# A mixed image and text block on one core: one run of scatters, unread products where TensorE waits, and a later place for three gates

## What is computed

```python
h = concat([tok(x), txt(x_txt)], axis=1)              # 32 x 68 x 256
h = h + attn(layernorm(h))
h = h + ffn(layernorm(h))
# attn
u = x @ W_x.T + b_x;  g = sigmoid(x @ W_g.T + b_g)     # hidden 512
u = u * g + conv3(u) * (1 - g)
dt = clip(softplus(x @ W_dt.T + b_dt).mean(axis=(0, 1)), 1e-3, 2)
A = -softplus(A_raw);  A_d = exp(A * dt);  B_d = (A_d - 1) / (A + 1e-6) * B_ssm
new = A_d * carry + B_d * u_t;  y_t = new . C_ssm      # 16 states, 68 steps
out = layernorm(x + y @ W_out.T + b_out)
# ffn: softmax router on a normalized row, the two best of four experts
hid = relu(layernorm(h @ w1[e]));  expert_out = hid @ w2[e]
out = layernorm(sum over the two best of weight * expert_out)
```

## Time and profile before

| | us |
|---|---|
| median of 3 runs (505.38 to 506.0) | 505.75 |
| the profiled execution | 506.89 |
| its span on the core | 505.1 |
| PE busy, share of the span | 440.4, 87% |
| DVE | 335.9, 66% |
| ACT | 299.7, 59% |
| POOL | 152.3, 30% |
| mean granted clock of TensorE | 0.935 |

### The profile page before, as it was taken

The page is one execution under the profiler, slowest core; times in us unless marked ns, Lnnn a source line. Parts: engine busy times, 40 slices in busy tenths (PEclk is TensorE's granted clock), DMA queues, the critical chain, the costliest instruction groups (busy, mean ns, idle before and its releaser), DMA issues.

```text
span 505.1 us, 9872 instructions
## 1 busy us (share of the span) xinstructions
PE 440.4 (87%) x3094; PEld 360.9 (71%) x3094; DVE 335.9 (66%) x980; ACT 299.7 (59%) x669; POOL 152.3 (30%) x255
## 2 busy tenths in 40 slices
PE   8989988697799999998998869999899999999500
PEld 5769967465678878886776657888778888888300
DVE  6876567788989125335787985876574666666584
ACT  2854368378866465225564533887596777877341
POOL 2000000000000000002245884874677645454322
PEclk9999999699799999988999958999999999999855
DMA  8981099800049942967212221232232243242262
GB/s 179 180 229 47 32 295 314 241 1 1 0 100 208 191 113 67 243 194 206 66 42 65 94 74 53 75 103 77 86 104 85 77 123 118 70 146 78 72 213 80
DMA packets 58734, 59.92 MB, mean 119 GB/s; under 512 B 25369, under 2 KB 51261, under 8 KB 57405
## 3 DMA queue, kind: packets, MB, share of 16 engines
q1 hardware_dynamic: 54236, 48.68, 37.1%
q0 software_dynamic: 3552, 9.74, 5.1%
q10 hardware_dynamic: 896, 0.89, 0.6%
HBM read 34.50 MB, written 24.80 MB: 117 GB/s over the span
## 4 chain that ended last, share of the span: by engine, by line
PE 70%; DVE 12%; ACT 8%; issue 5%; DMA 2%; another core or an unknown queue 1%; SPq 1%; POOL 0%; DVEq 0%; POOLq 0%; ACTq 0%
PE bank L1016 13%; PE bank L863 9%; PE bank L431 8%; PE bank L433 8%; PE bank L432 7%; PE bank L929 6%; PE bank L1006 3%; PE bank L883 3%; PE bank L911 2%; PE bank L923 2%; PE bank L988 2%; PE bank L954 1%; DVE spj L1380 1%; DMA got<-expert_y 1%; PE bank L933 1%
## 5 line engine op out<-in xcount | busy, mean ns | idle before, releaser
L1016 PE MATMUL bank<-w,hr 128*128 x320 | 76.1, 380 | 2.9 <-DVE ysb L1641 2.6
L1016 PEld LDWEIGHTS bank<-w,hr 128*128 128x128 f32 x320 | 59.9, 189 | 13.6 <-issue 4.5
L642 POOL MEMSET ones<- 2x128 f32 x1 | 0.2, 206 | 214.3 <-PE bank L898 214.3
L1214 ACT ACTIVATE hr<-bank,gsel 128x128 f32<-128x128 f32 x160 | 60.0, 460 | 0.2 <-PE bank L1006 0.2
L717 POOL DMA_INDIRECT expert_y<-ysb,toid x40 | 42.9, 1072 | 52.9 <-DVE ysb L1641 37.9
L863 PE MATMUL bank<-Tb,U 68*32 68x68 f32 x1024 | 46.3, 360 | 0.1
L863 PEld LDWEIGHTS bank<-Tb,U 68*32 68x32 f32 x1024 | 41.1, 141 | 3.4 <-issue 2.9
L1626 DVE BATCH_NORM_STATS2 bsth<-bank 128x6 f32<-128x512 f32 x40 | 27.7, 693 | 20.4 <-PE bank L433 15.0
L929 PE MATMUL bank<-Wo,yT 128*128 128x256 f32 x136 | 36.8, 418 | 2.4 <-ACT yT L1029 2.1
L669 POOL DMA_INDIRECT sorted_x<-x2s,slot x34 | 33.7, 991 | 16.7 <-issue 9.3
L1206 ACT ACTIVATE hn<-bank,nmrh,rsh 128x512 f32<-128x512 f32 x40 | 31.1, 779 | 10.0 <-DVE nmrh L1635 8.0
(11 more groups left out here) (296 smaller groups left out, 1154.7 us busy)
## 6 DMA issues: line engine op xcount, KB each, us to landing
Tb<-ssm_kernels SPq DMA_DIRECT2D x16, 680.0 KB, 9.2
sorted_x<-zpad SPq DMA_DIRECT2D x6, 1419.0 KB, 13.8
xg<-sorted_x SPq DMA_DIRECT2D x40, 129.0 KB
got<-expert_y SPq DMA_DIRECT2D x17, 256.0 KB, 3.7
XI<-in_x_dram SPq DMA_DIRECT2D x12, 288.0 KB, 5.4
h0r<-h_spill SPq DMA_DIRECT2D x17, 128.0 KB, 2.6
out_dram<-acc SPq DMA_DIRECT2D x17, 128.0 KB
w1raw<-in_L_ffn_w_dram SPq DMA_DIRECT2D x4, 512.0 KB, 15.5
```

The costliest lines, as they stand in the source:

```text
L1016: mm = pe.matmul(bank[6][:, 0:D], hr[:, i % 3, c, :], w2[:, bass.ds(expert[i], 1), c, :].rearrange("p o n -> p (o n)"), start=(c == 0), st ...
L1214: last = act.activation(hr[:, i % 3, c, :], bank[3 + i % 2][:, c * P:(c + 1) * P], ACT.Relu, scale=gsel[:, i, 0, c:c + 1], bias=gsel[:, i, ...
```

## The change

There are four edits. The number of DMAs and of products that are read stays the same.

1. In the sort, the tiles of a first-part group now lie 0.1 times as far apart for `scat` (`RUN`), so that each group's eight indirect DMAs are next to each other on POOL.
2. In the tile stage, `fill` gets new places (`FILLS`, and 3 ahead of the waits of `yT` 0 and `out` 0), and the 16 ahead of the first `b1` become 8.
3. `idle`, the same thing with other weights, stands 20 times before `project_dt(4)` and 14 times in chunk 1.
4. In chunk 1, ACT makes `u_parts` of blocks 0 and 1 and all four exponentials before its first `gate`, which leaves one table load where there were three; TensorE makes u of block 3 before g of block 2.

```diff
+        RUN = 0.1
@@ place_of
             elif kind == "scat":
-                n, late = RG[group_of(i)][-1] // 2, i - RG[group_of(i)][0]
+                first_part = group_of(i) < PART0_GROUPS
+                n, late = RG[group_of(i)][-1] // 2, (i - RG[group_of(i)][0]) * (RUN if first_part else 1)
@@ TensorE
+            pe.wait_ge(sem("v_init"), 4)
+            idle(bank[1], 20)
             for q in range(AHEAD, HC * NB):
                 project_dt(q)
             for step in C_STEPS:
+                if step == ("proj", 1, 2):
+                    project(1, 2, "u")
+                    project(1, 3, "u")
+                    pe.wait_ge(sem("dt_read"), HC * NB)
+                    idle(bank[4], 14)
+                    project(1, 2, "g")
+                    continue
                 if step[0] == "proj":
-                    project(step[1], step[2])
+                    project(step[1], step[2], "g" if step == ("proj", 1, 3) else "ug")
                     continue
...
+            FILLS = {("yT", 13): 2, ("out", 13): 3, ("x2T", 10): 7, ("yT", 14): 7, ("lgm", 11): 2, ("yT", 15): 2}
             for kind, i in order("pe"):
+                if (kind, i) in FILLS:
+                    fill(bank[3], FILLS[kind, i])
                 if kind == "yT":
                     if i == 0:
+                        pe.wait_ge(sem("w1_hi"), 1)
+                        fill(bank[3], 3)
...
                 elif kind == "out":
+                    if i == 0:
+                        fill(bank[3], 3)
...
                     if i == 0:
                         pe.wait_ge(sem("slot"), PART0_GROUPS)
-                        fill(bank[3], 16)
+                        fill(bank[3], 8)
@@ ScalarE
             u_parts(1, 0)
-            gate(1, 0)
-            act.preload_act_table_set("natural_log_exp_and_others")
+            u_parts(1, 1)
             for j in range(HC):
                 act.wait_ge(sem("adt"), j + 2)
                 act.activation(Eb[:, j], Eb[:, j], ACT.Exp).then_inc(sem("powers"), 1)
-                if j == 1:
-                    u_parts(1, 1)
             for step in C_STEPS:
                 if step[0] == "proj":
                     if (j, nb) not in ((1, 0), (1, 1)):
                         u_parts(j, nb)
-                    if (j, nb) != (1, 0):
-                        gate(j, nb)
+                    gate(j, nb)
```

More of the change, by code:

```diff
@@ L819, in _, with project @@
                     project_dt(step[1])
-            def project(j, nb):
+            def project(j, nb, kinds="ug"):
                 n0, w = BLOCKS[nb]
@@ L825, in project @@
                 for wt, first, done, read in ((1, 0, "u_mm", "v_init"), (2, 2, "g_mm", "gate")):
+                    if done[0] not in kinds:
+                        continue
                     if c >= 2:
@@ L839, in _, with idle @@
                 project(0, nb)
+            def idle(ps, count):
+                for _ in range(count):
+                    pe.matmul(ps[:], WT[0][0][:, 0, 0:P], WT[0][0][:, 0, :], start=True, stop=True)
+            pe.wait_ge(sem("v_init"), 4)
+            idle(bank[1], 20)
             for q in range(AHEAD, HC * NB):
@@ L956, in _ @@
                     if two(i):
-                        if i == 0:
-                            pe.wait_ge(sem("w1_hi"), 1)
                         fill(bank[3], 2)
```

## The result

The kernel after takes **497.29 us** (median of 4 runs, 496.07 to 498.21) where the one before takes 505.56 us in the same comparison (504.4 to 506.0). The ratio is 0.9847 with a 95% interval of 0.9817 to 0.9877: 8.3 us less (6 to 9 by the interval), where 7.3 were forecast.

A forecast was written before the change was run, and what follows sets the result against it. TensorE bounds the kernel from 306.3 us on, but earlier waits for DVE and ACT at partly half clock. Gates -2.2, twenty products +1.4, head -1.7, tile stage -4.8 sum to -7.3 us: 498.4 from 505.75, range 494.8 to 502.8.

The forecast's parts named there:

- The bound: From 306.3 to 476.8 us TensorE is busy at full clock, so time gained before 306 should reach the end.
- The twenty products: Before project_dt(4): 20 products delay the dt stage; 1.4 us lost, between 0 and 2.4 depending on the clock.
- The gates: Chunk 1: ACT's exponentials before its gates save two table loads; kT 2.2 us earlier, 14 unread products cost nothing.
- The Toeplitz loads: Behind kT in chunk 1: DVE's copy to kt becomes late itself, leaving 1.9 us earlier for these loads.
- The head: Tile stage's start: six unread products keep the clock up for the first two out; 1.7 us gained, or 0.
- The tile stage: Up to the first b1: 3.5 us from 16 to 8 and full clock, 1.3 from scatters; 4.8, from 3.4 to 5.7.
- the 1.3 of the forecast: Scatters in one run: DVE's r1 14 comes 0 to 2.1 us earlier, taken as 1.3 with faster out's 0.4 inside.
- The scheme of POOL's two runs: POOL in the tile stage: eight scatters, four additions, eight scatters, seven additions back to back to 299.5 us.
- The lock of DVE and POOL: Tile stage: by the skill, each DVE instruction waits for one POOL addition at most, 0.73 us; stage gain then 5.7.
- Only the 16 less 8 count: Rival: detour before dt costs 2.4 us, head's clock falls as before, r1 14 no earlier; 502.4 us, chance 0.21.
- The slower rival: Unread products become the bound if TensorE is at half clock near 290.4; 509.2 us, chance 0.07.
- Absorbed: Rival: POOL's table ends when it did, so TensorE's gain ends in waits for toid or gsel; 505.7 us, chance 0.04.

The follow-up runs named there:

- no_run: The kernel after with RUN = 1, so the first part's scatters are spread again: 499.01 us, ratio 0.9859 to before.
- no_twenty: The kernel after without the 20 unread products ahead of project_dt(4), the 14 in chunk 1 kept: 494.88 us, ratio 0.9815 to before.
- gates_alone: The kernel before with only ACT's new order in chunk 1 and u of block 3 moved, no unread products: 500.81 us, ratio 0.9942.
- after_again: The kernel after, unchanged, measured and profiled a second time as a control: 497.36 us, ratio 0.9861 to before.
- fills_alone: The kernel before with only the tile stage's unread-product edit (new places, 16 to 8), scatters still spread: 501.00 us, ratio 0.9924.
- the second set: The four runs no_run, no_head, no_front and early_add, measured beside runs of the kernel before at 506.57 us.
- early_add: The kernel after with the 20 products ahead of q = 8, POOL's h0b 12 ahead of the second scatter run, h0b 13 first behind: 499.28 us, ratio 0.9857.
- the three fastest kernels: The kernel after with the 20 ahead of q = 8 (493.01 us); also 2 products for the 8 (492.86); also two POOL additions moved (491.78).
- no_head: The kernel after without the 3 and 3 unread products ahead of yT 0 and out 0: 501.36 us, ratio 0.9895 to before.
- no_front: The kernel after with FILLS empty, without the 23 unread products in the waits of tiles 10 to 15: 503.07 us, ratio 0.9919.

## Why the prediction was right, and where it was not

**The bound.** "What comes earlier at 306 should come earlier at the end": confirmed by the pair without a standstill, 7.40 us at the first `b1` and 7.07 at the last product. Of the stretches at half clock ahead of it, though, the prediction names four, and the trace has a fifth, from 220.9 to 224.3 us; the second profile of the kernel before lacks it.

**The twenty products: the term was mis-sized.** The mechanism, the first short projection (88.8 forecast, 88.89 measured), the start of `q` = 8 (95.2; 95.33), the gap (3.7; 3.65) and the clock's fall behind it came as written. The size did not: +1.4 was taken between 0 and 2.4, and in the two pairs of profiles it is +2.5. The step that failed is the credit for `q` = 8 at half clock ("would lose some of these" waits): DVE waits 1.21 us for its first result in the kernel after the earlier trace rows, so nothing was won back by that wait. What is won back hangs on how long the clock stays low: in `no_run`, with 3.4 us and not 6.8, the stage ends 1.1 us sooner than in the kernel after, which is the forecast's +1.4. Against `no_twenty` the detour costs 2.9 us in the profiles and 1.6 to 2.3 by the ratios. The term's value lies between its middle and its upper end, mostly near the latter.

**The gates: mis-sized the other way.** Forecast -2.2, measured -4.3 from the end of dt to `kT`. Two steps of the sum were off. The last gate, counted from the end of dt, ends 2.9 us earlier than before, and not 1.8: the prediction priced a block on ACT at 1.33 + 0.70 = 2.03 us, and a gate follows the last after 1.82 (in the kernel before it was 1.80), and the part ahead of them was 0.5 us too long as well. The turns behind it take 1.4 us less than before, since they run at full clock, where the prediction had 0.7 at most for the clock and left it out of its 2.2. The 1.8 does stand in `gates_alone`, where the last gate starts 1.7 us earlier, but by luck: there ACT waits 0.93 us for products at half speed, which the forecast did not have. Of the 4.3, ACT's order gives 2.9 and the 14 products 1.5. The prediction priced them at "nothing": it asked only what they cost and not what the clock without them would do. The two table loads are 1.28 us each as before. The Trainium skill's 2.66 us per switch (ScalarE: Activation LUTs, "What ACT_TABLE_LOAD costs") would have made ACT's part 4.9 us; the isolated run shows 2.9 in all, so the trace still does not agree with it.

**The Toeplitz loads** were to be the next late thing (DVE late with its copy, 1.9 us left for them). DVE is late as forecast (waits 0.16 us, and is 1.74 us earlier from the end of dt). But TensorE's first `ssm` step keeps the whole 4.3 us, since TensorE's own queue stood ahead of it and not the load: the first 680 KB landed at 151.55 us and the step began at 152.17. Some of the 4.3 us is given back in the steps behind: from `kT` to `yT` 0 the kernel after takes 0.4 us more than before in the first pair (whose before had 3.4 us at half clock there) and 1.2 in the second. That loss stood in no term. So the forecast for `yT` 0, 0.8 us earlier (1.4 lost, 2.2 won), is met (1.4 and 0.7) by three errors that cancel: 2.5 lost, 4.3 won, 0.4 to 1.2 given back. The loss comes with the 14 products: every profile that has them takes 88.7 to 89.4 us there, `gates_alone` 88.0. Two new waits of TensorE are in it, 0.66 us ahead of a turn at 208 us and 0.29 ahead of an `ssm` step at 217 in `after_again`; the trace names no releaser for them, and the rest is not settled.

**The head.** Forecast -1.7; measured -1.8 and -1.4. The reason given, that the six products keep the clock up, is not confirmed: two profiles without them had the clock up too.

**The tile stage.** Forecast -4.8 (3.5 for 16 to 8 and the clock, 1.3 for the run). From `yT` 13 to the first `b1` it gained 5.7 and 6.0 us, and lost 1.0 and 0.65 between the head and `yT` 13: -4.7 and -5.4. `fills_alone` gives 3.9 of it (3.5 and the 0.4). The kernel after is 1.8 us better there, but the run of scatters taken back alone costs only 0.9 (`no_run` takes 16.93 us from `yT` 13 to the first `b1`, after 16.04), so the 1.3 of the forecast lies between two measurements, of which the one that isolates the run is the lower, and 0.66 go off ahead of `yT` 13. Eight products take 1.85 us (1.84 forecast), the turn 0.75 (0.69). The scheme of POOL's two runs came out as drawn, with tile 12's addition late and DVE waiting for it. Counted from the first scatter (271.18 and 268.37), the second pair of `ln1b` starts after 26.0 us where it was 28.2: 2.2 earlier, at the top of the forecast's 0 to 2.1.

**The lock of DVE and POOL.** The Trainium skill (SBUF — State Buffer, "Who interferes with whom") holds that a VectorE instruction with two SBUF inputs and a GpSimd one that reads SBUF contend for a shared port, which is an exclusive lock. The prediction took from it that DVE waits for one addition at most. In the kernel after this fits: beside a POOL that adds without pause two of DVE's long instructions take 1.36 and 1.74 us, and two of their like 0.87 alone, less than one addition more each; POOL's additions take 0.9 to 1.0 us there and 0.7 elsewhere. In the kernel before it does not fit. From its timeline, the second long instruction of `ln1b` 6, and POOL beside it:

```profile
295.93 3.42 DVE L1498 SCALAR_TENSOR_TENSOR r<-r,mv,lng_b 128x256 f32<-128x256 f32 x1
...
296.29 0.74 POOL L663 TENSOR_TENSOR h0r<-h0r,lnb_b 128x256 f32<-128x256 f32 x1
296.97 1.41 POOL L704 TENSOR_TENSOR h<-h,onb_b 128x256 f32<-128x256 f32 x2
298.33 0.73 POOL L663 TENSOR_TENSOR h0r<-h0r,lnb_b 128x256 f32<-128x256 f32 x1
```

One instruction of DVE is held through four additions in a row, and they keep their 0.7 us each. It is the same in `fills_alone` (3.43 us) and `gates_alone` (3.44). In `no_run` it is held for 2.75 us, through three additions, until POOL pauses for 0.4. So a string of additions with no scatter between them can hold DVE whole, or the two can take turns, and what decides which was not isolated.

**Rivals.** "Only the 16 less 8 count" was right in one clause, the detour's 2.4, and wrong in the two that carried it. The slower rival decided by the clock at 290.4, which was full in both profiles of the kernel after. "Absorbed" had POOL's `table` as the new wait; none came.

## What to carry to other kernels

Put unread products only into a wait that the trace shows at that very place, and count them at full price anywhere else: the same twenty cost 1.6 to 2.9 us ahead of four short steps and gained 1.8 us behind them. Price a filler in a wait by two sums, what it costs and what the clock does without it, since the second can be the larger, and follow the gain to the end of the next stage: of the 1.5 us that the 14 products gave at `kT`, 0 to 0.7 were left 88 us later. When steps are bunched on an engine, look at what now stands behind the bunch: with one addition of 0.7 us moved ahead of the run and one to its end, the first `b1` came 1.3 us sooner, and the median was 1.1 us lower, which the intervals do not resolve.

## What the runs showed of the hardware

**A standstill of three engines.** In some profiles TensorE, DVE and ACT start nothing for 0.4 to 1.1 us while POOL goes on, TensorE's own gap is 1.4 to 1.7 us, and the instruction of ACT that ends it has no releaser on the core. The kernel before has one near 364 us, all four of the second set have one at 356 to 363, at the same instruction, and such gaps of TensorE between 276 and 293 as well. Here `early_add`, ACT, timeline:

```profile
292.44 0.38 ACT L1057 ACTIVATE xT<-bank 128x256 f32<-128x256 f32 x1 [2.79 <-remote]
```

Both profiles of the kernel after, the repeated one of before and the three fastest kernels lack it, and no view names its cause. It went with 1.8 us in a comparison of two profiles, a fifth of their difference.

**A low clock ahead of every edit.** Four of the profiles (`fills_alone`, `no_head`, `no_front`, `early_add`) have TensorE at 1.2 GHz from about 34 to 38 us, where the program is the same in all, and are 1.5 us late at the first short result of dt. TensorE's gap just ahead is the same 1.43 us in the kernel before, where the clock stays up. Eight profiles have it low for 3.4 us somewhere between 213 and 226 us; in the kernel before it is from 220.9 to 224.3, and TensorE had no gap over 0.12 us in the 10 us ahead of it. These cost nothing that the landmarks show. An effect of 1.5 us read from one profile has to be looked for stage by stage.
